# Gated attention with a mixture of experts on one core: batch 1's query and key projections in the prologue, probability buffers doubled, products with v in sets of two key chunks

## The reference

```python
xn = layernorm(x)
q, k, v = xn @ Wq + bq, xn @ Wk + bk, xn @ Wv + bv        # 8 heads of 16
attn = softmax(q @ k.T / 4)                               # per batch and head, 512 x 512
o = attn @ v[head % 4] - lam * attn @ v[4 + head % 4]     # lam from four small vectors
s = 0.2 * (layernorm(o) * ln_w + ln_b) @ Wo + bo
h = int(xn[:, 0] + xn[:, 1]) % 8                          # each token goes to experts h and h+1
f = 0.5 * sum over its two experts of (relu(xn @ W1[e] + b1[e]) @ W2[e] + b2[e])
out = x + s * silu(f)
```

## Time and profile before

| what | us |
|---|---|
| median of 3 runs | 457.02 (456.78 to 457.38) |
| the profiled execution's own time | 457.09 |
| its span, first to last instruction | 455.0 |
| PE busy | 406.6 (89%) |
| DVE, ACT, POOL busy | 337.2, 236.0, 127.5 |

### The profile page before, as it was taken

How to read it: one execution, slowest core, us unless ns; L and a number is a source line. 1 busy time by engine, 2 the same in 40 slices (tenths; PEclk the granted TensorE clock), 3 DMA queues, 4 the chain that set the end, 5 groups by cost and what they waited for, 6 DMA issues and landing times.

```text
span 455.0 us, 8683 instructions
## 1 busy us (share of the span) xinstructions
PE 406.6 (89%) x2672; PEld 251.9 (55%) x2672; DVE 337.2 (74%) x936; ACT 236.0 (52%) x543; POOL 127.5 (28%) x154
## 2 busy tenths in 40 slices
PE   1917889999999999898999999999999999998683
PEld 1314666565666757575656757575666657552122
DVE  6788785767687777687677777787787876867954
ACT  4550435555645545564546554564555555556670
POOL 5701142233231411424123151243242222200101
PEclk9955999999999999999999999999999999999996
DMA  7998243232703144303604145211806430345220
GB/s 253 306 297 269 85 132 131 72 123 59 262 23 120 48 134 153 124 16 105 220 14 175 42 127 172 98 55 38 260 22 187 141 127 14 126 132 182 99 75 23
DMA packets 36805, 57.34 MB, mean 126 GB/s; under 512 B 6350, under 2 KB 24376, under 8 KB 36762
## 3 DMA queue, kind: packets, MB, share of 16 engines
q1 hardware_dynamic: 28937, 49.19, 32.0%
q0 software_dynamic: 2496, 5.12, 4.3%
q10 hardware_dynamic: 5328, 2.49, 2.0%
HBM read 14.02 MB, written 6.75 MB: 46 GB/s over the span
## 4 chain that ended last, share of the span: by engine, by line
PE 71%; DVE 12%; issue 5%; ACT 5%; DMA 4%; POOL 1%; ACTq 0%; POOLq 0%; DVEq 0%
PE ring L1180 13%; PE pv_bank L1125 12%; PE score L1084 12%; PE ring L1195 12%; PE exp L1113 10%; DVE neg_max L842 4%; PE ring L1050 3%; DMA xs<-xn_rows,inverse 2%; PE ring L1149 2%; PE ring L1171 2%; PE ring L1133 1%; ACT xn L625 1%; PE ring L1073 1%; DVE stats_o L889 1%; DMA xn_rows<-xn 1%
## 5 line engine op out<-in xcount | busy, mean ns | idle before, releaser
L650 ACT ACTIVATE probs<-exp 128x512 f32<-128x512 f32 x244 | 141.6, 600 | 121.8 <-PE exp L1113 118.5
L842 DVE TENSOR_REDUCE neg_max<-score 128x1 f32<-128x512 f32 x256 | 172.2, 685 | 30.3 <-PE score L1084 19.9
L1084 PE MATMUL score<-ks,qs 96*128 96x512 bf16 x256 | 98.9, 390 | 10.8 <-DVE neg_max L842 10.1
L1113 PE MATMUL exp<-qs,ks 99*128 99x512 bf16 x244 | 92.1, 381 | 3.3 <-ACT probs L650 1.4
L584 POOL DMA_INDIRECT y_rows<-y_sb,y_row x39 | 39.7, 1018 | 188.8 <-DVE y_sb L974 188.4
L1180 PEld LDWEIGHTS ring<-xsT,pair 128*128 128x128 f32 x624 | 80.3, 193 | 15.4 <-issue 10.2
L1180 PE MATMUL ring<-xsT,pair 128*128 128x128 f32 x624 | 84.7, 279 | 0.6 <-issue 0.6
L1195 PEld LDWEIGHTS ring<-w_sb,hT 128*128 128x128 f32 x624 | 74.6, 192 | 5.9 <-issue 1.7
L1195 PE MATMUL ring<-w_sb,hT 128*128 x624 | 77.6, 277 | 0.0
L672 ACT ACTIVATE hT<-ring,pair 128x128 f32<-128x128 f32 x172 | 49.2, 370 | 45.6 <-PE ring L1180 43.8
L1125 PE MATMUL pv_bank<-probs,va 128*32 128x512 f32 x512 | 68.2, 605 | 0.8 <-ACT probs L650 0.7
(11 more groups left out here) (150 smaller groups left out, 345.7 us busy)
## 6 DMA issues: line engine op xcount, KB each, us to landing
pair<-table SPq DMA_DIRECT2D x39, 580.0 KB
qs<-parts SPq DMA_DIRECT2D x48, 128.0 KB
ks<-parts SPq DMA_DIRECT2D x48, 128.0 KB
w_sb<-in_L_ffn_W_dram ACTq DMA_DIRECT2D x9, 256.0 KB
s_sb<-_attn_hidden_states_dram SPq DMA_DIRECT2D x8, 256.0 KB, 5.7
table<-in_L_ffn_W_dram SPq DMA_DIRECT2D x2, 1024.0 KB, 9.9
xn_rows<-xn SPq DMA_DIRECT2D x8, 256.0 KB
table<-_attn_hidden_states_dram SPq DMA_DIRECT2D x8, 256.0 KB, 4.6
```

The lines of the kernel that those rows point to most:

```text
L650: a.activation(probs[:, n % PR, :], exp_banks[n][:, :], ACT.Exp, scale=SCALE).then_inc(exp_done, 1)
L842: v.tensor_reduce(neg_max[:, b % 2, col:col + 1], score_bank[n % 2][:, :], AX.X, ALU.max, negate=True).then_inc(max_taken, 1)
L1084: t.matmul(score_bank[n % 2][:, :], qs[0:MAX_ROW, b % STK, hh, c * P:(c + 1) * P], ks[0:MAX_ROW, b % STK, hh, :], start=True, stop=True).t ...
L1113: t.matmul(exp_banks[n][:, :], ks[0:KROWS, b % STK, hh, kc * P:(kc + 1) * P], qs[0:KROWS, b % STK, hh, :], start=True, stop=True).then_inc ...
```

## The change

It does six things.

1. Batch 1 joins `PEELED`: its transpose, projections and peels stand in the prologue (times -50 to -45.2), its middle and low parts are made by PE and ACT instead of DVE and POOL, into a buffer of their own inside `probs` (`early_parts`). Its 12 stackings are issued by SP at times 12.1 to 12.6, after the first tile's result (`y_ready`).
2. `probs` has 16 buffers: 8 as before and 8 in the memory of the input `xin`, which no longer shares memory with `s_sb`; `s_sb` now lies over `xn`, and the gates are loaded back (`load_y`) into slot 2 of `qs` and `ks`.
3. A pv step takes two key chunks: eight matmuls instead of four in a row, at every eighth score step. The last two chunks stay single.
4. In the prologue, b2 and b1 are loaded by ACT's queue ahead of the bias loads, spread by PE as its first work (`bias_rows`, into the score and exp banks) and copied by ACT alone; POOL makes `xn` of batches 4 to 7; SP issues the last weight load and the ten small loads before, not after, six of the eight stores of `xn_rows`; ACT's nine weight loads are spread over the list.
5. Both routing steps stand together, `tile_experts` is done for three tiles ahead of the inverse and for the others after it, `y_row` is computed behind it, and the last group of `find_rows` is 4 rows, not 8. SP's first pair waits for those three tiles' experts and no longer for `inverse`; `at_row` and `token` lie outside `pair`.
6. The lambda product is moved to time 4.2 and the folding that needs it from 9 to 6.5 (`bias_o` from 14.1 to 11.6).

The diff, cut to its core:

```diff
-PR = 8
+PR = 16
+PV_GROUPS = 2
+PV_TAIL = 2
-POOL_NORM = (6, 7)
+POOL_NORM = (4, 5, 6, 7)
-NORM_AT = (-58, -56.4, -55.2, -48, -47.9, -47.8, -49, -48.9)
+NORM_AT = (-58, -56.4, -49.9, -47.93, -49.2, -49.1, -49, -48.95)
-QKV_AT = (-57.9, 4, 40, 72, 104, 136, 168, 186)
-PEELED = (0,)
-PROJECT_AT = ((-55.9, -55.6),)
+QKV_AT = (-57.9, -50, 40, 72, 104, 136, 168, 186)
+PEELED = (0, 1)
+PROJECT_AT = ((-55.9, -55.6), (-47.95, -45.9))
+PEEL_AT = (((-55.5, -55.3), (-55.4, -55.25)), ((-45.5, -45.3), (-45.4, -45.2)))
+STACK_AT = (((-55.58, -55.45, -55.28), (-55.57, -55.35, -55.2)), ((12.1, 12.3, 12.5), (12.2, 12.4, 12.6)))
-B2_AT = -48.5
-ROUTE_AT = (-47, -46, -40.5)
+BIAS_AT = -58.2
+BIAS_COPY_AT = -45.45
+ROUTE_AT = (-48.8, -48.7)
+EXPERTS_AT = (-40.5, -39.9)
+FIRST_TILES = 3
-W2_AT = -47.2
-B1_AT = -46.5
-W1_LAST_AT = -47.6
-SMALL_AT = -47.4
-ONES_AT = -47.1
+Y_ROW_AT = -39
+W2_AT = (-49.85, -49.8, -49.75, -47.92, -47.91, -47.9, -45.85, -45.8, -45.48)
+W1_LAST_AT = -50.2
+SMALL_AT = -50.1
+ONES_AT = -45
-FOLD_AT = 9
+LAMBDA_AT = 4.2
+FOLD_AT = 6.5
-ROW_GROUPS = 4
+ROW_ENDS = (10, 20, 28, 32)
...
-            if n % 4 == 3:
-                at(n + LAG + PV_OFF, "pv", n // 4)
+            if n % 4 == 3 and n // 4 >= PV_STEPS - PV_TAIL:
+                at(n + LAG + PV_OFF, "pv", n // 4, 1)
+            elif n % (4 * PV_GROUPS) == 4 * PV_GROUPS - 1:
+                at(n + LAG + PV_OFF, "pv", n // 4 - PV_GROUPS + 1, PV_GROUPS)
...
-        probs = sb("probs", [P, PR, S])
+        probs = sb("probs", [P, PR // 2, S])
+        early_parts = probs[:, 2:2 + PARTS, :].bitcast(BF16).rearrange("p j (i n) -> p i j n", n=S)
...
-        s_sb = sb("s_sb", [P, NT, D])
-        xin = s_sb
+        s_sb = xn
+        xin = sb("xin", [P, NT, D])
+        more_probs = xin[:, :, :].rearrange("p t d -> p (t d)").rearrange("p (r n) -> p r n", n=S)
...
                 elif kind == "stack_part":
                     b, i, k = s[1:]
                     sp.wait_ge((high_ready, mid_ready, low_ready)[k], 2 * b + i + 1)
+                    if b == 1:
+                        sp.wait_ge(y_ready, 1)
...
                     if f == 0:
                         sp.wait_ge(texp_ready, 1)
-                        sp.wait_ge(inverse_ready, 1)
                         sp.wait_ge(expert_loaded, 16 * 3)
-                        sp.wait_ge(table_ready, 2)
-                        sp.wait_ge(b1_ready, 1)
+                        sp.wait_ge(table_ready, 1)
+                    if f == FIRST_TILES:
+                        sp.wait_ge(texp_ready, 2)
...
                 elif kind == "exp":
                     n = s[1]
                     act.wait_ge(exp_filled, n + 1)
+                    if n == 2:
+                        act.wait_ge(stacked[1], 12 * 16)
                     if n >= PR:
-                        act.wait_ge(pv_done, (n - PR) // 4 + 1)
-                    a.activation(probs[:, n % PR, :], exp_banks[n][:, :], ACT.Exp,
+                        act.wait_ge(pv_done, n // 4 - PR // 4 + 1)
...
+                    a.activation(prob(n), exp_banks[n][:, :], ACT.Exp,
...
-                elif kind == "b2":
-                    i = s[1]
+                elif kind == "bias_rows":
                     pe.wait_ge(b2_loaded, 16 * 3)
-                    free(uses[s])
-                    t.matmul(shared[:, :], ones[0:2, :], b2_rows[:, FF * i:FF * (i + 1)],
-                             start=True, stop=True).then_inc(shared_filled, 1)
+                    for i in range(2):
+                        t.matmul(score_bank[i][:, :], ones[0:2, :], b2_rows[:, FF * i:FF * (i + 1)],
+                                 start=True, stop=True)
+                    pe.wait_ge(b1_loaded, 16)
+                    t.transpose(exp_bank[0][:, 0:EXP * FC], b1_rows[:, :],
+                                ident[0:EXP * FC, 0:EXP * FC]).then_inc(bias_filled, 1)
...
                 elif kind == "pv":
-                    n4 = s[1]
-                    grp, kc = divmod(n4, C)
-                    b = grp // 2
-                    pe.wait_ge(exp_done, 4 * n4 + 4)
...
+                    first, groups = s[1:]
+                    pe.wait_ge(exp_done, 4 * (first + groups))
+                    for n4 in range(first, first + groups):
+                        grp, kc = divmod(n4, C)
...
+                        for i in range(HALF):
+                            last = t.matmul(pv_bank[VW * i:VW * (i + 1), :], va[:, b % 2, kc, i, :],
+                                            prob(4 * n4 + i), start=(kc == 0), stop=(kc == C - 1))
+                    last.then_inc(pv_done, groups)
```

More of the change, by code:

```diff
@@ L129, in schedule @@
     at(FOLD_QK_AT, "fold_qk")
-    at(W2_AT, "load_w2")
+    for expert in range(EXP + 1):
+        at(W2_AT[expert], "load_w2", expert)
     at(ONES_AT, "ones")
```

154 lines of the change are left out of this document (83 added, 71 removed).

## The result

The changed kernel is slower: 463.51 us (median of 4 runs, 459.29 to 464.51) against 457.20 before (4 runs, 456.78 to 458.13), a ratio of 1.011 with a 95% interval of 1.0065 to 1.0155: a loss of about 1%, clear of zero and small. I had forecast 449.0 and given "slower" 6 in 100. The profiled execution took 463.7 with a span of 461.9, 6.9 more than before.

What follows compares the result with a forecast made beforehand. The prediction took PE's own work to bound some 330 us of the kernel. 457.1 - 3.2 (earlier first exp) - 4.9 (merged pv sets) = 449.0 us, own range 447 to 451.5, wider range 445.5 to 453.5 leaving out 0.2.

Steps and rivals of the forecast that it cites:

- Inverse, -1.3: Prologue routing: `inverse`, written at 38.28 before, comes at 37.0, a gain of 1.3 us.
- Batch 1 out: Tile stage, 38 to 70: batch 1's 3.7 us of chain pieces go; first exp 3.2 earlier, including 1.3 from `inverse`.
- (d): SP's prologue queue: stores of `xn_rows` go out at about 29 to 31, land by 36.9, level with `inverse`; cost 0.
- The inverse or its gather is late: Rival for the prologue: batch 1's PE work cold throughout, or stores landing last, delays `inverse` or the first gather; chance 0.15.
- it lands before the gather and no longer ends a wait: First pair load at the start: waits for three tiles' experts, lands before the gather; counted inside the 1.3 us gain.
- 26 x 0.19 = -4.9: Product with v, 80 to 410: 26 merges of two sets gain 0.19 us each on average, 4.9 in all.
- In the last 45 us: 0: Behind the tiles, where DVE sets the pace, merged pv sets gain nothing: 0 us.
- (c) POOL: Prologue: eight more normalizations on POOL, 3.83 us from 22.4 to 26.3, do not lengthen DVE's instructions; cost 0.
- The merge pays nothing: Rival for the pv sets: a 2 us block starves DVE and PE waits as much as it saved; 453.9 us, chance 0.12.
- little of it works: Rival for the whole: a late prologue and a merge without gain, 457 give or take 1 us; chance 0.05.
- Slower: each merge costs a full wait: Rival for the pv sets: PE waits at a score while DVE is in the tile's relu, 26 times; 463 us, chance 0.05.
- The clock stays up: Rival for the start: new prologue work on PE carries the full clock into the scores, saving some 3 us; 446, chance 0.13.

Runs made afterwards that it cites:

- the fastest kernel: Changed kernel with stores first, pv sets merged, pairs issued two units earlier and DVE's bursts moved for groups 0 to 13: 444.76 us, ratio 0.9737 to the kernel before.

## Why the prediction was wrong, step by step

**Inverse, -1.3: right.** Written at 36.40 against 38.10, -1.7; but 0.5 of that is a routing that began sooner in this execution (L859 at 17.74, the same step of before at 18.26), and against the second profile of before (37.41) it is -1.0. From that step on, `inverse` came 1.0 to 1.2 sooner.

**Batch 1 out: right in size at the start, not seen in the whole.** I put 1.9 of the 3.2 on it (3.2 less 1.3) with a bound of 3.7; it measured 2.5 (77.2 to 74.7), and with the stores first the start came 2.1 to 3.4 earlier than in the two profiles of before. But I carried it to the end of the kernel, and no run bears that out: batch 1 late was the faster both with the stores late (460.80 against 463.51) and with the stores first (457.48 against 460.48). With the stores first the wait at 186 and two falls of the clock between 30 and 230 took it back; only the wait goes with the early batch in every profile. The 3.2 also held a deduction for the clock, which I let come back later because PE does less ahead of the first *hidden*. No run shows that: with the stores first it was back at 47.7 with batch 1 early and at 48.6 with batch 1 late.

**"(d) … that is 36.9: level with the new inverse, nothing to spare … I cost all five at 0": wrong.** This is the first step that failed. I let the stores go out "at about 29 to 31"; eleven issues before them took 8.2 us, one 2.70, so the last went out at 33.97. I used 5.73 for its landing; it took 6.65. It landed at 40.6, 4.2 us after `inverse`. A cover without a margin was costed as a cover. The rival "The inverse or its gather is late" named the stores, and was priced, at up to 2.4, for the wrong mechanism (batch 1's matmuls at half pace throughout: from 22.5 to 32.4 their pairs of f32 passes took 0.99 to 1.13, where batch 0's took 1.02 in the kernel before at 17.91, and the granted clock stayed at 1.00 until 37.8). The start came 1.5 late instead of 3.2 early: with the next step, 4.7 off.

**"it lands before the gather and no longer ends a wait. Inside the -1.3": wrong.** Three pairs issued at 38.39, beside the last store and just ahead of the gather, stretched the gather from 3.82 to 5.61 and the first turned tile by 2.1 (pairs held back). In the earlier trace rows they were issued behind it, and I asked only when they were needed, not what they would share the transfers with. Nor did the pair cease to end a wait: with the stores first it was issued at 40.12 and landed 3.20 later, and the first *hidden* waited for it until 43.36.

**"-0.19 on average, as PE waits for DVE so seldom there: 26 x 0.19 = -4.9": wrong, and the largest miss.** The price of a merge was right: a set of 16 holds PE 1.85 to 1.94 against twice 1.10, and PE was occupied 4.3 us less over 25 merges in 30 to 230, 0.17 each; 5.1, 0.20 each, where DVE no longer interferes (307.2 to 302.1). Wrong was the reason that waits were seldom. They were seldom *because* a pv set stood at each burst. Taking out the set at 14.5 uncovered DVE, and 4.0 us came back as waits: 2.2 for maxima, 1.2 for pairs and gathers that were just in time before. I had weighed DVE's slack as an average (83 us of 330) and the order of its maxima around a set, but never the steps that stand at the same time as the set that I removed. Five kernels measure this: merged without cover 0.3 us of gain (316.5 to 316.2), bursts moved with single steps 4.9, both together 11.3 (315.3 to 304.0), so 6.4 for the merge. The first was taken with the pairs late and the others with the pairs early; the merged kernel with early pairs and the bursts in place wasn't run. By its waits (1.2 more for pairs and gathers than with single steps) it would have gained some 1.5, an estimate, so most of the 6.4 is the cover's but not all.

**"In the last 45 us: 0": wrong.** 230 to the end took 4.5 more (66.1 against 61.6), most of it by the clock: 3.4 us at 0.50 from 413.3 and 6.8 from 433.8. PE was busy 3.40 and 5.14 of them, and half of that, 4.3, is an estimate of what they cost; longer waits (2.06 for 1.36, new ones of 0.48 and 0.54) and the merges saved there about cancel. I put the term at nothing from DVE's pace alone and left out the clock over the end and the waits of 1.36 and 1.68 there. Across the runs the end behind score 255 follows the clock: 32.2 with none of it (two profiles), 33.6 to 33.8 with 3.4 us, 34.8 to 35.5 with 6.8. The one exception is the profile at 0.95, 34.7 with 3.4 us. The 24 us behind score 255's maxima, before, with single steps and stores first, and as changed:

```profile
422.70:446.70 24.00, 16.51 (x102) 5.26 (x100) 17.24 (x47) 14.88 (x28) 1.40 (x3) 1.00 0.21 78
```

```profile
419.90:443.90 24.00, 18.06 (x102) 5.54 (x100) 15.92 (x39) 14.88 (x28) 1.32 (x2) 0.93 0.21 78
```

```profile
426.50:450.50 24.00, 18.77 (x105) 5.97 (x105) 15.24 (x38) 14.38 (x28) 1.32 (x2) 0.86 0.21 78
```

The same 102 matmuls take 16.51 at 1.00 and 18.06 at 0.93.

A small slip in the sum of this term: twice 0.86 + 0.23, less 1.10, is 0.85 and not 0.88, so a merge behind the tiles would have cost 0.03 and not 0.06; nothing hangs on it.

**16 buffers, 0; (c) POOL, 0: right.** No wait for `pv_done` came up, and `inverse` was early with eight more normalizations on POOL. DVE's route from L793 to `find_rows` took 7.50 against 7.32 before, so it was held up 0.2 at most: on DVE the trace sided with the row. The upper edge of my range, 453.5, allowed for most of a late `inverse`; no run shows one held up over POOL, and in the changed kernel it was written 1.7 sooner than before. But I had looked at one side only. Five of POOL's sixteen normalizations took 0.61 to 0.81 where the others took 0.45 to 0.50, each of the five beside DVE instructions of 256 columns with both inputs in SBUF (L781, L786, L788, L804, L806; one more, beside the first 0.22 of L786, took 0.45); in the kernel before it was one of eight (0.69, beside L735). The five took 3.45 together, against 2.25 at 0.45 each. On DVE, L788 and L806 took 0.49 and 0.48 beside them, where L742 and L760, the same steps of before with POOL idle, took 0.43 and 0.42. So here POOL, which sets no pace, bore most of it.

**The rivals.** "The merge pays nothing" (0.12) and "the gather is late" (0.15) both came true; together with the end they make the loss: 457.1 + 1.5 + 0.9 + 4.5 is 464.0, where the profiled execution took 463.7. I had joined them only as "little of it works", 457, with 0.05. "Slower: each merge costs a full wait" gave 463, near the result, by another sum: its mechanism, PE at a score while DVE is elsewhere, was there, but in four places (64, 160, 208, 239) and not 26, and behind other steps than the relu. "The clock stays up" came half true: 1.00 until 37.8, where before had fallen at 23.8, but then 0.50 to 51.5, and before only to 47.7.

**What stays open** is what makes the clock fall at the end. It isn't the change as a whole, since the kernel before with moved bursts shows it, nor the large sets. Nor do the idle gaps alone decide it: single steps have 1.37 and 1.67 there and fell; before has 1.36 and 1.68 and didn't. And the gaps of 1.76 and 1.93 behind which the kernel with the stores first lost the clock stand in the changed kernel as 1.36 and 1.94, with no fall. It varies by execution too. In 30 executions of the kernel before, 13 had a mean clock of at least 0.965 and a median of 455.93 (454.73 to 457.06), 17 had less and 458.09 (456.82 to 461.41). Each of the falls between score 30 and the last 10 us stands in or behind an idle gap of PE, the shortest of 1.03 us (changed kernel, 412.3) and the longest of 5.8 (bursts moved, 405.0), but no run here tells which gaps suffice. No kernel was tried that fills the gaps at the end. Open too is why the early batch brings the wait at 186, and whether it pays at all in the fastest kernel, of which no version with batch 1 late was run.

## What to carry to other kernels

Before you shorten or merge a block on the engine that sets the pace, list what the second engine does during each such block: a bank that is rarely waited for may be so because that block covers a burst. Then move the burst under a block that stays; here that was worth 4.9 us by itself in that stretch (some 3 of it went again at the end), and with the pairs early it turned the merge from 0.3 into 6.4. On a queue that gates a stage, put what gates it first, count every issue ahead of it at its worst row, and don't start a large prefetch beside the store or gather that the stage waits for (5.61 us against 3.82 for the gather here); after each move look again at what passed it on the queue, as the gate loads did (9 to 10 us). Judge each part by the whole time and not only by the stage that it shortens: the early batch gained 2.5 us at the start, and no whole time shows them. A cover of nothing to spare is a cost with a chance of one half, not zero.

## What was not expected of the hardware

- A single issue of a small load on SP took 2.70 us where its neighbours took 0.43 to 0.77; which of the eleven was slow changed from run to run (1.59 and 1.35 in the run with held pairs).
- A DRAM gather issued behind two SBUF-to-SBUF pairs and within 0.15 us of a third took 5.4 to 5.6 us, one issued just ahead of the pairs 3.82 (pairs held back), one behind two of them with the third 1.2 us later 3.71 (batch 1 late). A pair amid twelve stackings took 6.13 in one kernel and 3.93 in another.
- From score 30 to the last 10 us the granted clock fell, mostly for 3.4 or 6.8 us, only during idle gaps of PE of over 1.6 us or up to 1.6 us behind gaps of 1.0 to 2.1 us, but not at each such gap. One execution (every second pair merged) ran at 0.95 from 80 to 400.
- Five of POOL's normalizations took 0.61 to 0.81 us beside DVE instructions of 256 columns with two inputs in SBUF, and the other eleven 0.45 to 0.50 (the changed kernel).
